# Products of ones in front of four waits of TensorE, in an eight-block transformer kernel

## What is computed

```python
x = x + xattn0(layernorm(x), ctx, mask)      # 16 heads of 32, softmax over 77 keys
x = x + ternary_ffn(layernorm(x))            # rows quantised to 8 bits, weights -1, 0, 1
x = x + xattn1(layernorm(x), ctx)            # 16 heads of 64, softmax, output projection
x = x + spectral_ffn(layernorm(x))           # fft, a sparse complex matrix, inverse fft
```

## Time and profile before

| | |
|---|---|
| median of 3 runs | 1040.56 us (1039.41 to 1041.71) |
| profiled execution | 1040.61 us, span 1037.5 us |
| mean granted TensorE clock | 0.967 of full speed |
| TensorE busy with matmuls | 897.2 us (86%), 6236 matmuls |
| VectorE, ScalarE, GpSimd busy | 835.0, 648.9, 579.0 us |

### The profile page before, as it was taken

One profiled execution on the slowest core, in us unless ns is written; L12 is line 12 of the kernel. 1 busy time (PEld: TensorE's weight loads), 2 busy tenths in 40 slices (PEclk: granted clock), 3 DMA queues, 4 the chain that ended last, 5 costly groups with the idle time before them and its releaser, 6 DMA issues.

```text
span 1037.5 us, 17964 instructions
## 1 busy us (share of the span) xinstructions
PE 897.2 (86%) x6236; PEld 495.0 (48%) x6236; DVE 835.0 (80%) x1451; ACT 648.9 (63%) x1808; POOL 579.0 (56%) x588
## 2 busy tenths in 40 slices
PE   0799798978679988998899899989999998799587
PEld 0447574544335544554445445545554454444343
DVE  7997869799887898789978997899788968845724
ACT  2538853676865696669666966796578746525710
POOL 3306664543654678467747774776478636715513
PEclk9999999988889999999999999999999999899989
DMA  8871669594757566847593858485857554622605
GB/s 290 144 174 29 129 137 158 159 226 94 139 85 150 83 127 109 196 74 134 104 201 68 151 99 194 80 146 100 186 95 132 106 132 82 123 41 65 115 8 162
DMA packets 352904, 130.39 MB, mean 126 GB/s; under 512 B 333487, under 2 KB 342640, under 8 KB 349999
## 3 DMA queue, kind: packets, MB, share of 16 engines
q1 hardware_dynamic: 352815, 129.25, 61.0%
HBM read 33.57 MB, written 15.96 MB: 48 GB/s over the span
## 4 chain that ended last, share of the span: by engine, by line
PE 36%; DVE 27%; ACT 11%; POOL 10%; DMA 7%; issue 6%; SPq 3%; ACTq 0%; DVEq 0%; POOLq 0%
PE wb L264 10%; PE wb L265 10%; PE wb L266 10%; ACT pr L1039 5%; DMA prT<-ph 4%; POOL pr L885 3%; DVE xh L1320 3%; PE wb L1581 3%; DVE ph L1402 3%; DVE parts L1117 2%; ACT xh L1064 2%; DVE mx L1382 2%; DVE xr L1336 2%; POOL xr L911 2%; POOL xn L900 2%
## 5 line engine op out<-in xcount | busy, mean ns | idle before, releaser
L885 POOL TENSOR_TENSOR pr<-pr,sm 128x616 f32<-128x616 f32 x128 | 177.8, 1389 | 225.9 <-DVE sm L1397 225.9
L1039 ACT ACTIVATE pr<-scores,bound,factor 128x77 f32<-128x77 f32 x576 | 230.5, 420 | 8.5 <-POOL ph L890 2.1
L264 PE MATMUL wb<-xT,wq_hl 128*128 128x512 f16 (+1 forms) x400 | 151.5, 379 | 15.5 <-DMA xT<-xh 8.2
L265 PE MATMUL wb<-xT,wq_hl 128*128 128x512 f16 (+1 forms) x400 | 151.4, 378 | 0.0
L266 PE MATMUL wb<-xT,wq_hl 128*128 128x512 f16 (+1 forms) x400 | 151.2, 378 | 0.0
L1052 ACT ACTIVATE ph<-pr 128x618 f16<-128x618 f32 x128 | 93.5, 731 | 46.6 <-POOL pr L885 33.2
L1039 ACT ACTIVATION_READ_ACCUMULATOR pr<-scores,bound,factor 128x1 f32 x576 | 119.5, 207 | 0.0
L264 PE MATMUL wb<-wo_hl,qc 128*128 128x512 f16 x276 | 105.6, 383 | 5.5 <-DVE x L1336 3.2
L266 PE MATMUL wb<-wo_hl,qc 128*128 128x512 f16 x276 | 105.6, 383 | 0.0
L265 PE MATMUL wb<-wo_hl,qc 128*128 128x512 f16 x276 | 105.6, 383 | 0.0
L1320 DVE TENSOR_TENSOR xh<-xn,xh 128x1024 f16<-128x1024 f32 x48 | 76.9, 1601 | 22.7 <-ACT xn L1067 9.4
(11 more groups left out here) (232 smaller groups left out, 2443.0 us busy)
## 6 DMA issues: line engine op xcount, KB each, us to landing
xr<-in_x SPq DMA_DIRECT2D x6, 1024.0 KB, 5.9
out_x<-xr SPq DMA_DIRECT2D x5, 1024.0 KB, 5.1
xr<-in_wk SPq DMA_DIRECT2D x3, 1024.0 KB, 6.9
xr<-in_wq SPq DMA_DIRECT2D x3, 1024.0 KB, 10.2
xr<-in_wv SPq DMA_DIRECT2D x3, 1024.0 KB, 5.7
k1b<-scr_k SPq DMA_DIRECT2D x16, 154.0 KB, 4.3
scr_k<-k1b SPq DMA_DIRECT2D x7, 308.0 KB, 5.9
x<-in_x SPq DMA_DIRECT2D x2, 1024.0 KB, 7.3
```

The lines of the kernel that those rows point to most:

```text
L264: pe.matmul(out, lhs(0), rhs(0), start=start, stop=False, **kw)
L265: pe.matmul(out, lhs(0), rhs(1), start=False, stop=False, **kw)
L885: pool.tensor_tensor(v, v, s, ALU.mult).then_inc(probs_ready, 1)
L1039: ins = act.activation(pr[U % 3][:, h // 4, cols], sc[:, U % 2, h // 4, cols], ACT.Exp, bias=bound[:, U % 2, h:h + 1], scale=k["factor"][: ...
```

## The change

A table `WARM` names four fills or units, and a number for each. Ahead of them TensorE gets `in_step`: it waits until the bank of the next fill is free and then makes that number of products of ones by ones (stationary 128x128, moving 128x512, the 128 columns read four times over) into that bank. They signal nothing, and the next fill overwrites the bank. For a fill, the products stand directly ahead of it; for a unit, directly ahead of its scores, in the bank of the fill that TensorE will make next. Two semaphores are declared and used nowhere.

```diff
+WARM = {("Y", "pv", 4, 0): 9, ("Y", 6, 6): 12, ("Y", 6, 7): 8, ("Z", "out", 0, 7): 4}
...
+NEXT_FILL = [sum(len(v) for v in SLOT_FILLS[:g]) for g in range(len(SLOTS))]
...
+        wk1_second, wv1_second = sem("wk1_second"), sem("wv1_second")
...
+            def in_step(use, n):
+
+                if n >= WB:
+                    pe.wait_ge(bank_free, n - WB + 1)
+                for _ in range(WARM[use]):
+                    pe.matmul(wb[:, n % WB, :].rearrange("p (c n) -> p c n", c=4), ones[:, :],
+                              ones[:, :].rearrange("p (c n) -> p c n", c=1).broadcast_to([P, 4, P]), start=True, stop=True)
+
             pe.wait_ge(zeroed, 1)
             for g, (i, s) in enumerate(SLOTS):
                 follows = unit_at(g + 1)
                 if follows and follows[:2] != ("Y", 0):
+                    if follows in WARM:
+                        in_step(follows, NEXT_FILL[g])
                     scores(*follows)
                 for use in SLOT_FILLS[g]:
+                    if use in WARM:
+                        in_step(use, FILL[use])
                     fill(use)
                 if follows and follows[:2] == ("Y", 0):
+                    if follows in WARM:
+                        in_step(follows, NEXT_FILL[g + 1])
                     scores(*follows)
```

## The result

The change makes the kernel slower by 0.47%: median 1044.04 us over 20 runs (1040.88 to 1050.72), against 1039.51 us over 20 runs before (1034.74 to 1042.70). The ratio is 1.0047, 95% interval 1.0035 to 1.0059. The forecast was 1040.6 us and no difference, and the measured loss is clear of zero. At the places that it looked at, though, the trace shows much of what it described. The loss comes from somewhere that it never looked.

The account below looks back on a forecast made before the run. No engine was taken as the bound everywhere (TensorE 36% of the chain, VectorE 27%); at the four places others start later than TensorE ends. The terms summed 0 + 0 + 0 + 0 = 0 us, giving 1040.6 us, range 1038.2 to 1042.8.

Parts of the forecast that it names:

- The change part by part: At all four places: 33 added products fit in TensorE's waits, weight loads lie beside them, cost taken as 0 us.
- place A: ("Y","pv",4) of block 0: nine products in a 4.58 us wait, 2.6 us left idle, 0 us at the end.
- The slower rival: Longer waits before block 6's ("Y","pv",4) and block 0's output make the clock fall: together 2.9 us slower; chance 0.25.
- B: ("Y",6) of block 6: twelve products mostly hold the clock, 1.95 us recovered on TensorE, 0 us at the end.
- C: ("Y",6) of block 7: eight products mostly hold the clock, 1.7 us recovered on TensorE, 0 us at the end.
- D: ("Z","out",0) of block 7: four products, 0.9 us in a 1.50 us wait; nothing recovered, nothing lost.
- The faster rival: At the recovered low stretches: time reaches the end, 5.35 us for all three, 1.7 to 1.95 for one; chance 0.23.

Follow-up runs that it names:

- e1_declared: Changed kernel with an empty WARM table, only the new declarations: 1036.85 us against 1037.68 for the kernel before, ratio 0.9991.
- e4_block7: Changed kernel with only the last block's products, eight before ("Y",6) and four before ("Z","out",0): 1035.77 us against 1037.68 before, ratio 0.9989.
- e3_block6: Changed kernel with only the twelve products before the scores of ("Y",6) of block 6: 1039.28 us against 1037.68 before, ratio 1.0010.
- e2_first: Changed kernel with only the nine products before ("Y","pv",4) of block 0: 1043.21 us against 1037.68 before, ratio 1.0051.
- e16_earlier: Whole change plus 119 four-column products before ("Y","pv",0) of block 0: 1038.78 us against 1036.83 before, ratio 1.0020.
- e9_turn: Changed kernel with only 128 four-column products (256 instructions) before ("Y","pv",4) of block 0: 1040.88 us against 1038.17 before, ratio 1.0020.
- e12_short: Changed kernel with only 119 four-column products (238 instructions) before ("Y","pv",4) of block 0: 1041.43 us against 1038.17 before, ratio 1.0022.
- e14_sixteen: Changed kernel with only sixteen full products, before ("Y","pv",4) of block 7: 1035.83 us against 1036.83 before, ratio 0.9988.

## Why the prediction was wrong

**The step that failed** is in "The change part by part": the 33 products were costed by the time that they fill in four waits, and their weight loads as lying beside them, and everything between block 0 and block 6 was taken to stay as it was. The step put at nothing that they are instructions in a stream that has to be brought in. Eighteen of them in block 0 shift what each of the 37 later instruction loads holds, and from block 3 on transposing DMAs land late. What the runs showed in place of its 0: +0.51% for place A alone, and +0.09% and +0.20% when the same change is filled up to a whole load. The row was there to be read, on the page before: 49 loads on the instruction queue. That the price is not that of the products' own work, these two kernels show: they make all 33 products and most of the loss is gone. How the shift delays the DMAs stays open.

**Place A by itself** went nearly as forecast: 2.68 us of idle left, and of the half of the low stretch that was counted on at most, nothing was saved. The output behind it waits 0.72 us for VectorE's parts, 0.77 before, where the slower rival had 2.5:

```profile
319.80 0.38 PE L266 MATMUL wb<-wo_hl,qc 128*128 128x512 f16 x1 [0.72 <-DVE qc L1330]
```

**B and C** went as forecast. The clock held, TensorE's time was recovered, and at B VectorE's maximum came no sooner; B alone measures 1.0010, C and D together 0.9989.

**D** was no loss either: the last low stretch had moved but ended at 1004.4, the four products ran at the upper clock, and 0.53 us of the wait was left, where 0.6 had been forecast.

**The slower rival** (the longer wait in front of ("Y","pv",4,6), then a fall) had the sign right, and its mechanism shows in the trace after, at 7.11 - 5.76 = 1.35 us where 1.2 had been worked out. But it is not the cause of the loss: place B alone, which has all of it, measures 1.0010, and at most 1.0024 by its interval, and everything but A 1.0012. That this rival pointed to the right side is luck. Whoever reads only the trace after would settle on it. How the falls come and go is what the prediction quoted from the Trainium skill ("TensorE: Matmul & The Clock Gate", Part 1: The HAM clock gate), that one kernel shows differing numbers of slow matmuls from run to run. The traces of this case agree as far as they go: with the same products up to block 7, the fall around B is in `e1_declared` (884.1 to 891.0 us) and in `e4_block7` (882.6 to 889.4) as in the earlier trace rows, but the stretch at 907.8 of the earlier trace rows is in neither, and `e1_declared` has one at 576.9 to 580.3 that the other two do not have.

**The faster rival** needed recovered time to reach the end. `e3_block6`'s trace has it once (36 products in 4.08 us), and its ratio over all runs does not show it.

**The range** of 1038.2 to 1042.8 was built from the four places alone, and the median of 1044.04 lies above it. A cause outside the places had no share in it.

**Still open:** whether it is the instruction loads themselves that delay the transposing DMAs, and how (a shared DMA engine is a guess; it wasn't tried), or something else that goes with the step of 256; how the 5 us split over the places behind block 3, where the trace of `e2_first` gives 1.4 + 1.7 us in block 3 and the rest in small steps; why the tiny products cost less than the full ones (1.0023 and 1.0025 for 18 instructions, 1.0051 and 1.0059 with full products), if that is more than scatter; and whether the 0.2% of `e16_earlier`, `e9_turn` and `e12_short` is the price of 119 to 128 tiny products or scatter.

## What to carry to other kernels

An instruction that costs nothing on its engine may still cost by being there: where the page shows an instruction queue with loads during the run, every insertion shifts what all later loads hold, so an early insertion should be timed alone, and timed again with the stream filled up to a whole load. Find that out before you explain a loss by the places that you edited. A stretch at the lower clock is worth treating only where TensorE ends the wait that follows; and where the clock falls while the fillers run, they can take as much as the clock gives back (2.07 us of 2.03 in `e14_sixteen`).

## What the runs showed of the hardware that was not expected

- TensorE's instructions came in loads of 16.3 KB, 49 to 51 a run, one for about 256 instructions, most of them taking 0.9 to 1.5 us. A transposing DMA of the kernel before lands 3.7 us after its issue (median of 128), but in 16 cases only after 4.9 us or more (up to 6.7) in the trace before, and in 24 cases after, 12 of the 16 and 20 of the 24 with such a load in their time. Of the other DMAs 30 of 112 and 21 of 104 had one.
- With eight to eighteen more instructions early on the ratios are 1.0023 to 1.0059; with 256 more they are 1.0009 to 1.0020. For tiny products alone the two do not separate (1.0023 and 1.0025, 1.0020).
- Unread products of ones hold the clock as real ones do (1.00 behind the waits at B and C, with 1.54 and 1.46 us of idle left); at A, with 2.68 us left, the clock fell all the same.
- Products of 4 columns: nine in 0.36 us.
